# A new slot pipeline for two graph-attention layers: scores two chunks ahead, values two behind

## The reference

```
h = relu(layernorm(x)); x = x + L0(h, adj)      # scores q.k/sqrt(32) + beta*adj, masked where adj <= 0
h = relu(layernorm(x)); x = x + L1(h, adj)      # scores q.k/sqrt(384) + adj, then @ Wo.T + bo
q = h @ Wq; k = h @ Wk; v = h @ Wv              # L0 with biases on q, k, v; L1 with W.T and a bias on v
out = softmax(scores) @ v                        # L1: rows whose scores are all 0 give 0
```

## Time and profile before

| | |
|---|---|
| median of three runs | 2788.24 us |
| profiled execution: span from first to last instruction | 2786.6 us |
| PE busy | 2492.9 us, 89% |
| DVE busy | 2035.5 us, 73% |
| ACT busy | 2045.4 us, 73% |
| POOL busy | 1205.5 us, 43% |
| share of the DMA queue of SP (q1) | 33.7% |

### The profile page before, as it was taken

The page is one execution under the profiler, slowest core; times in us unless marked ns, Lnnn a source line. Parts: engine busy times, 40 slices in busy tenths (PEclk is TensorE's granted clock), DMA queues, the critical chain, the costliest instruction groups (busy, mean ns, idle before and its releaser), DMA issues.

```text
span 2786.6 us, 78169 instructions
## 1 busy us (share of the span) xinstructions
PE 2492.9 (89%) x20772; PEld 1447.7 (52%) x20772; DVE 2035.5 (73%) x10864; ACT 2045.4 (73%) x7824; POOL 1205.5 (43%) x1543
## 2 busy tenths in 40 slices
PE   3699999999999999999999999999999999999976
PEld 2355555555555555555555555555555555555543
DVE  3477777777777777777777777777777777777756
ACT  2577777777777777777777777777777777777765
POOL 1344444454444444444444444444444444444431
PEclk8899999999999999999999999999999999999988
DMA  3333333333333333333333333333333333333321
GB/s 118 90 89 87 93 94 87 95 102 86 88 96 86 94 103 86 86 97 87 94 102 88 85 99 86 94 100 89 83 99 88 95 98 90 82 99 91 78 55 45
DMA packets 164279, 251.27 MB, mean 90 GB/s; under 512 B 29776, under 2 KB 114768, under 8 KB 163920
## 3 DMA queue, kind: packets, MB, share of 16 engines
q1 hardware_dynamic: 163920, 248.11, 33.7%
HBM read 71.83 MB, written 25.17 MB: 35 GB/s over the span
## 4 chain that ended last, share of the span: by engine, by line
PE 45%; ACT 17%; DVE 16%; issue 16%; POOL 3%; SPq 1%; ACTq 1%; DVEq 1%; DMA 0%; POOLq 0%
PE job_bank L765 21%; ACT probs L479 12%; PE pt_bank L792 9%; PE o_bank L807 4%; PE misc_bank L832 4%; DVE neg L575 4%; PE score_bank L781 2%; PE misc_bank L846 2%; DVE stats L603 2%; ACT h_hi L516 2%; ACT probs_t L493 2%; PE misc_bank L868 1%; ACT qk L531 1%; DVE h_lo L700 1%; POOL part_lo L420 1%
## 5 line engine op out<-in xcount | busy, mean ns | idle before, releaser
L479 ACT ACTIVATE probs<-neg,neg_max 128x128 f32<-128x128 f32 x3072 | 1185.5, 390 | 9.4 <-DVE neg_max L575 9.4
L493 ACT ACTIVATE probs_t<-pt_bank 128x512 f32<-128x512 f32 x768 | 458.2, 597 | 567.7 <-PE pt_bank L792 516.5
L406 POOL TENSOR_TENSOR rstd<-shift_var,minus_half 128x1 f32<-128x1 f32 x256 | 152.2, 595 | 1020.3 <-DVE shift_var L612 1020.3
L479 ACT ACTIVATION_READ_ACCUMULATOR probs<-neg,neg_max 128x1 f32 x3072 | 583.9, 190 | 0.0
L792 PE MATMUL pt_bank<-ident,probs 128*128 128x128 f32 x3072 | 476.1, 278 | 57.5 <-ACT probs L479 42.9
L420 POOL TENSOR_TENSOR part_lo<-qk,part_hi 128x512 f16<-128x512 f32 x384 | 459.1, 1205 | 115.6 <-DVE part_hi L710 115.6
L792 PEld LDWEIGHTS pt_bank<-ident,probs 128*128 128x128 f32 x3072 | 362.7, 141 | 238.9 <-ACT probs L479 154.8
L765 PE MATMUL job_bank<-h_hi,w_hi 128*128 128x512 f16 x1152 | 441.4, 383 | 43.9 <-ACT qk L531 25.4
L765 PE MATMUL job_bank<-h_lo,w_hi 128*128 128x512 f16 x1152 | 438.5, 381 | 0.0
L765 PE MATMUL job_bank<-h_hi,w_lo 128*128 128x512 f16 x1152 | 438.0, 380 | 0.0
L575 DVE CUSTOM_DVE_ANT_0 neg<-score_bank,bias 128x128 f32<-128x128 f32 x1536 | 352.8, 285 | 103.3 <-issue 98.6
(11 more groups left out here) (69 smaller groups left out, 3949.8 us busy)
## 6 DMA issues: line engine op xcount, KB each, us to landing
stack<-part_hi SPq DMA_DIRECT2D x1024, 96.0 KB, 2.2
stack<-part_lo SPq DMA_DIRECT2D x512, 96.0 KB, 2.2
x_norm<-in_x SPq DMA_DIRECT2D x32, 768.0 KB, 4.5
x_res<-in_x SPq DMA_DIRECT2D x32, 768.0 KB, 4.7
out_x<-result SPq DMA_DIRECT2D x128, 192.0 KB, 1.9
adj<-in_adj SPq DMA_DIRECT2D x64, 256.0 KB, 2.9
stack<-in_L_gnn_Wq SPq DMA_DIRECT2D x2, 576.0 KB, 8.1
stack<-in_L_gnn_Wk SPq DMA_DIRECT2D x2, 576.0 KB, 8.9
```

What stands on the lines that cost most here:

```text
L406: pool.tensor_tensor(rstd[:, :], shift_var[:, b % 2, 1:2], minus_half[:, :], ALU.pow).then_inc(rstd_done, 1)
L479: last = act.activation(probs[c % 2][:, h, :], neg[c % 2][:, h, :], ACT.Exp, bias=neg_max[:, b, first + h:first + h + 1], scale=-1.0, accu ...
L493: act.activation(probs_t[c % 2][:, :, :].rearrange("p h q -> p (h q)"), pt_bank[c % 2][:, :], ACT.Copy).then_inc(probs_t_ready, 1)
```

## The change

Every engine's list of slots is rewritten; the arithmetic stays in the same form, apart from what is named here.

- PE: scores of chunk s+2 instead of s+1, the turn of chunk s-1 instead of s, and values of chunk s-2 instead of s-1. The mm of the projection are counted out per slot by a table (`PROJ`, one list for phases that attend layer 0, one for layer 1) and laid in three parts between the other work. The output projection comes at the slot's end.
- ACT: the exponentials of chunk s come first, the copy of chunk s-1 behind them. `part_hi` is written straight from PSUM at the slot's end. It also copies the turned inverse sums (`inv_t`) and writes `o_hi`; the copy `o_t` goes to DVE.
- DVE: `part_lo` straight from PSUM (one instruction instead of the cast), `o_t` or `o_norm` straight from `o_bank`, one instruction fewer for rows that are all zero, two instructions for layer 0's bias instead of three, built now in slot 11 of the layer-0 phase instead of slot 7 of the layer-1 phase.
- POOL no longer makes `part_lo`.
- PSUM: one `pt_bank` instead of two; `post_bank` and `h_bank` instead of `misc_bank`.
- Norms are at slots 0, 2, 4 and 6, turned two slots later and split three slots later, so that two are under way at a time.
- Scales: layer 0's weights for q and k are scaled by 16 instead of 256, and the factor is taken back in the scores.
- Start: layer 1's weights come already turned from the host, `x` and the first three matrices are loaded first, and the first phase of norms stands between the splits of the weights.

```diff
+PROJ = ((7, 7, 7, 6, 7, 7, 7, 6, 9, 9, 9, 9), (5, 8, 8, 4, 7, 8, 5, 9, 12, 6, 9, 9))
+MATMULS = 3 * KC
+
+NORM_SLOTS = (0, 2, 4, 6)
...
+    def counts(self):
+        return PROJ[self.attend.layer if self.attend is not None else 0]
+
+    def parts(self, s):
+
+        if self.project is None:
+            return (), (), ()
+        first = sum(self.counts()[:s])
+        todo = [divmod(m, MATMULS) for m in range(first, first + self.counts()[s])]
+        one = (len(todo) + 2) // 3
+        if s == SLOTS - 1:
+            one = (len(todo) + 1) // 2
+        return todo[:one], todo[one:2 * one], todo[2 * one:]
+
+    def jobs_done(self, s):
+
+        if self.project is None or s < 0:
+            return []
+        return [j for part in self.parts(s) for j, m in part if m == MATMULS - 1]
...
+                    u, b = finished(p, s, 5)
+                    if of_layer(u, b, 1):
+                        sp.wait_ge(result_ready, u.group * GROUP + (b + 1))
+                        sp.dma_start(out[u.group * GROUP + b, :, :], result[b][:, :]).then_inc(stored[b], 16)
+                    for j in p.jobs_done(s - 1):
+                        if j == KC - 1 or j == QK_JOBS - 1:
+                            stack(p.project, j // KC)
+                    if s == 6 and p.tail is not None and p.tail.layer == 0:
...
+            def high_part(u, j):
+                n = u.n * QK_JOBS + j
+                t = j // KC
+                act.wait_ge(job_done, u.n * JOBS + (j + 1))
+                if j % KC == 0 and some((u.half + u.parity) * STACK_DMAS * 16):
+                    act.wait_ge(stack_in[t][1 - u.parity], (u.half + u.parity) * STACK_DMAS * 16)
+                if u.layer == 0:
+                    last = act.activation(part_hi[t][:, j % KC, :], job_bank[j % 2][:, :], ACT.Identity,
+                                          scale=1.0, bias=b_cols[t][:, j % KC:j % KC + 1])
+                else:
+                    scale = (SCALE[1] if t == 0 else 1.0) / W_SCALE
+                    last = act.activation(part_hi[t][:, j % KC, :], job_bank[j % 2][:, :], ACT.Copy, scale=scale)
+                last.then_inc(part_hi_ready, 1)
...
+                    u, b = finished(p, s, 3)
+                    if of_layer(u, b, 1):
+                        act.wait_ge(inv_turned, u.group * GROUP + (b + 1))
+                        if some(u.group * GROUP + b):
...
+                        act.activation(inv_t[:, :, :].rearrange("p c q -> p (c q)"), post_bank[:, 0:DIM],
+                                       ACT.Copy).then_inc(inv_t_ready, 1)
+                    u, b = normed_in(p, s, 3)
+                    if u is not None:
+                        act.wait_ge(h_turned, u.n * GROUP + (b + 1))
...
+                        act.activation(h_hi[u.parity][:, :, P * b:P * (b + 1)],
+                                       h_bank[:, 0:DIM].rearrange("p (c n) -> p c n", c=KC),
+                                       ACT.Relu).then_inc(h_hi_ready, 1)
+                    if p.attend is not None:
+                        exponentials(p.attend, s)
                     u, c = unit_of_chunk(p, s - 1)
                     if u is not None:
...
-                        act.activation(probs_t[c % 2][:, :, :].rearrange("p h q -> p (h q)"), pt_bank[c % 2][:, :],
+                        act.activation(probs_t[c % 2][:, :, :].rearrange("p h q -> p (h q)"), pt_bank[:, :],
                                        ACT.Copy).then_inc(probs_t_ready, 1)
-                    if p.attend is not None:
-                        exponentials(p.attend, s)
-                    u, b = finished(p, s, 1)
...
-                    if p.project is not None and 1 <= s < 1 + 2 * KC:
-
-                        u, j = p.project, s - 1
-                        n = u.n * 2 * KC + j
-                        act.wait_ge(job_done, u.n * JOBS + (j + 1))
...
-                            last = act.activation(qk32[j % 2][:, :], job_bank[j % 2][:, :], ACT.Copy, scale=scale)
-                        last.then_inc(qk32_ready, 1)
...
+                    u, b = finished(p, s, 3)
+                    if of_layer(u, b, 1):
+                        act.wait_ge(o_norm_ready, u.group * GROUP + (b + 1))
+                        if some(u.group * GROUP + b):
+                            act.wait_ge(out_done, u.group * GROUP + b)
+                        act.activation(o_hi[:, :, :], o_norm[:, :, :], ACT.Copy).then_inc(o_hi_ready, 1)
+                    for j in p.jobs_done(s):
+                        if j < QK_JOBS:
+                            high_part(p.project, j)
+
+            high_weights(0, 3)
+            phase(before()[0])
+            high_weights(3, WEIGHTS)
+            act.wait_ge(cols_ready, 3)
+            run_phases(act, phase, 1)
...
+            def low_part(u, j):
+                t = j // KC
+                dve.wait_ge(part_hi_ready, u.n * QK_JOBS + (j + 1))
+                if u.layer == 0:
+                    last = dve.scalar_tensor_tensor(part_lo[t][:, j % KC, :], job_bank[j % 2][:, :],
+                                                    b_cols[t][:, j % KC:j % KC + 1], part_hi[t][:, j % KC, :],
...
             def phase(p):
-
-                bias_slot = SLOTS - 1 if p.attend is not None and p.attend.layer == 0 else 7
+                bias_slot = SLOTS - 1 if p.attend is not None else 7
                 for s in range(SLOTS):
+                    u, b = finished(p, s, 3)
+                    if of_layer(u, b, 0):
+                        dve.wait_ge(pv_done, chunk(u, b * KC + KC - 1))
...
+                        dve.tensor_copy(o_t[:, :, :].rearrange("p c q -> p (c q)"),
+                                        o_bank[:, 0:DIM]).then_inc(o_taken, 1)
+                    if of_layer(u, b, 1):
+                        dve.wait_ge(pv_done, chunk(u, b * KC + KC - 1))
+                        dve.wait_ge(inv_t_ready, u.group * GROUP + (b + 1))
+                        if some(u.group * GROUP + b):
+                            dve.wait_ge(o_lo_ready, u.group * GROUP + b)
+                        dve.tensor_tensor(o_norm[:, :, :].rearrange("p c q -> p (c q)"), o_bank[:, 0:DIM],
+                                          inv_t[:, :, :].rearrange("p c q -> p (c q)"),
+                                          ALU.mult).then_inc(o_norm_ready, 1)
+                    for j in p.jobs_done(s - 1):
+                        if j < QK_JOBS:
+                            low_part(p.project, j)
+                        else:
+                            take_v(p.project, j - QK_JOBS)
                     if p.bias is not None and s == bias_slot:
                         build_bias(p.bias)
-                    if p.project is not None and s in (8, 9, 11):
-                        take_v(p.project, {8: 0, 9: 1, 11: 2}[s])
                     u, c = unit_of_chunk(p, s + 1)
...
-                    if p.project is not None and 1 <= s < 1 + 2 * KC:
-
...
-                        dve.tensor_copy(part_hi[j // KC][:, j % KC, :], qk32[j % 2][:, :]).then_inc(part_hi_ready, 1)
-                    if p.project is not None and s == 11:
...
+                    u, b = normed_in(p, s, 0)
+                    if u is not None:
+                        norm_stats(u, b)
+                for j in p.jobs_done(SLOTS - 1):
+                    take_v(p.project, j - QK_JOBS)
...
             def phase(p):
                 for s in range(SLOTS):
-                    u, c = unit_of_chunk(p, s + 1)
+                    one, two, three = p.parts(s)
+                    u, c = unit_of_chunk(p, s + 2)
                     if u is not None:
                         scores(u, c)
-                    parts = range(3 * s, 3 * s + 3) if s < 2 * KC else range(2 * s + 6, 2 * s + 8)
-                    if p.project is not None:
-                        for part in parts[:1]:
-                            project(p.project, part)
+                    u, b = finished(p, s, 4)
+                    if of_layer(u, b, 0):
+                        turn_rows(u, b)
+                    for j, m in one:
+                        project(p.project, j, m)
                     u, c = unit_of_chunk(p, s - 1)
                     if u is not None:
+                        turn_probs(u, c)
+                    for j, m in two:
+                        project(p.project, j, m)
+                    u, c = unit_of_chunk(p, s - 2)
+                    if u is not None:
                         weigh_values(u, c)
+                    for j, m in three:
+                        project(p.project, j, m)
                     u, b = finished(p, s, 4)
-                    if u is not None and u.layer == 1:
-
-                        if p.norm is not None and some(p.norm.n * GROUP + s // KC):
-                            pe.wait_ge(h_lo_ready, p.norm.n * GROUP + s // KC)
-                        pe.wait_ge(o_hi_ready, u.group * GROUP + (b + 1))
-                        pe.wait_ge(o_lo_ready, u.group * GROUP + (b + 1))
```

(25 more changed lines are left out.)

479 lines of the change are left out of this document (213 added, 266 removed).

## The result

| | before | changed |
|---|---|---|
| median, us | 2788.03 (2783.97 to 2789.91, 4 runs) | 2914.82 (2912.14 to 2915.7, 4 runs) |
| span of the profiled execution, us | 2786.6 | 2912.2 |
| a turn of the loop / 28 turns / outside it, us | 83.45 / 2336.5 / 450.1 | 88.74 / 2484.7 / 427.5 |
| PE, DVE, ACT, POOL busy, us | 2492.9, 2035.5, 2045.4, 1205.5 | 2539.8, 2073.5, 2055.3, 719.3 |

The changed kernel is slower: ratio 1.0454, 95% interval 1.0439 to 1.0469. The forecast was 2777 us in a range of 2690 to 2835. Both halves missed to the same side: a turn takes 88.74 us where 84.4 stood (28 x 4.34 = 121 us), and outside the loop 23 us were won where 38 stood.

The account below looks back on a forecast made before the run. The path from k's last job through the stack's DMAs to the scores bounds each phase, plus clock falls: 84.4 us a turn. From 2786.6, +27 in the loop and -38 outside give 2775.6, +1.6 around the span: 2777 us, range 2690 to 2835.

Parts of the forecast that it names:

- The ring: From k's last projection job through 12 stack DMAs to slot 10's scores: sets phase length, PE waits 4.3 and 2.8 us.
- The clock: PE's clock falls behind each wait for the stack, costing 1.25 us per wait, bounds 0 and 1.7.
- Rival (a): PE waits for the stack, but 3 to 4 us don't lower its clock: about 2700 us, chance 0.20.
- VectorE in the layer-1 phase: Late negated scores in slots 2 to 5 and slot 7's output row add 1.4 us, bounds 0 and 4.
- rival (b): DVE paces the layer-1 phase and delays SP's k stack; 1.7 us more a turn gives 2825 us, chance 0.16.
- Layer-0 phase, slots 0 to 2: DVE grows to some 31 of 41 us in this phase and delays nothing, so no time was added.
- Outside the loop: Start, norm-only phases, last unit and six other phases together: -38 us.
- The start: Before the loop, norms beside weight loading and splitting, no weights turned on PE: -21 us, between 0 and -27.
- The six phases in the loop's manner: Phases outside the loop that follow the ring and its clock: +3 us, between -15 and +10.
- the two that only norm: Two phases outside the loop, two norms under way at once, 19 us to about 14: -10, between 0 and -16.
- the last unit: Attended without projection outside the loop, 43 us before: -10 us, between 0 and -16.
- Rival (c): Stacks don't bind through a shorter path to landing; PE bounds a turn at 73.4 plus 1.6 us: 2500 us, chance 0.12.

Follow-up runs that it names:

- e1: Changed kernel with projection matmuls dealt 9,9,9,9,9,9,6,6,6,6,6,6, so k's last job ends in slot 5 instead of 7: 2617.7 us, turn 79.3.
- e5: Changed kernel with TensorE's scores one chunk ahead instead of two, the new dealing kept: 2620.5 us, turn 79.3.
- e9: e6 with SyncE issuing the stack's 12 DMAs ahead of the output's DMA in slots that have both: 2708.8 us, turn 82.0.
- e2: Changed kernel with 60 and 36 extra 128x128 matmuls on TensorE in slot 10, ahead of its wait for the stack: 2800.8 us, turn 84.8.
- e4: Changed kernel without layer 1's row-wise absolute maximum on VectorE: 2810.8 us, turn 85.4.
- e6: Changed kernel with projection dealt 8,8,8,8,8,8,6,7,7,7,7,8 in both phases, so k's last job ends in slot 6: 2859.1 us, turn 86.7.
- e10: Changed kernel with its loop turned by one phase, so the back edge lies ahead of the phase with layer 1's attention: 2909.9 us, turn 88.7.
- e12: Changed kernel with the edits of e1 and e5 together, old dealing and scores one chunk ahead: 2595.5 us, turn 78.6.

## Why the prediction was wrong

- **The ring: right.** The waits stand where they were put, 4.2 and 2.9 us for 4.3 and 2.8, the path from issue to scores is 9.4 us in the layer-0 phase and 9.7 in the layer-1 phase for 9.4. e1 and e5 open it by two different edits, and e9 does so in the layer-1 phase.
- **The clock: the mechanism right, the size short. This is the first term of the sum that failed.** "I take 1.25 us for each wait; the bounds are 0 and 1.7" gave 2.5 us a turn; e2 measured 3.96, of which 2.1 stood behind the longer wait and 1.6 behind the shorter. The step took the 3.4 us at half speed of the earlier trace rows as the most there is. At the wait of 4.2 us it was 6.8 us in 17 of 20 turns; in the one shown 2.2 of them lie in the wait and 4.6 behind it. This is +1.5 us a turn. Rival (a) is refuted: the clock falls behind 2.9 us too. The Trainium skill, TensorE: Matmul & The Clock Gate, section "HAM oscillation — how this bites in real kernels", describes a loop in which the wait for a DMA brings the clock down anew each time; the trace agrees, in every turn and at both waits. The waits of 1.6 us in e5, as regular, did not bring it down.
- **VectorE in the layer-1 phase: right place, half the size. This is the second.** 1.4 us were put down, within 0 to 4; 2.9 were measured, and taking 7 us of its load away gives just these back (e4). Of the grounds named, the load was right and the output row wrong: it held the stack by 0.2 us, though in e6 it does so by 5.1. This is +1.5, near the 1.7 that rival (b) named; (b) alone would have given 2825.
- **Layer-0 phase, slots 0 to 2: the third, put at nothing.** "DVE grows to some 31 of 41 us and delays nothing": +1.05 us, although it is busy only 27.8. About 0.6 of it went when the back edge was moved (e10). The three terms make 4.0 of the 4.3 us.
- **Outside the loop.** -23 for -38. The start was near its -21: the first projection comes at 23.2 us instead of 53.0, and the first scores, now a slot earlier, at 58.4 instead of 79.7. The six phases in the loop's manner had +3; at half of a turn's miss, 2.2 us each, they account for 13 of the 15. e1 points the same way: with the ring open 394.7 us lie outside the loop instead of 427.5. How the shortfall divides between these phases, the two that only norm and the last unit was not traced.
- **Rival (c)** was right on what an open ring is worth in kind but not in size: the turn is 78.6 and not 75, and PE then waits 3.5 us in it for VectorE's output rows (e12).
- **What the prediction never asked** is what the change would be without its dealing. The three misses add up because they lie on one chain: in a closed ring each late step lengthens the phase in full. Why all three went to the same side the runs don't say; VectorE's 1.4 stood low in bounds of 0 to 4, and the third had no bounds.

## What to carry to other kernels

Before spreading work evenly, find which of it starts a slow path (here twelve DMAs, 10 us from job to landing) and put that part first; with scores two chunks ahead the even spread cost 297 us (25 with one), and the old front-loaded dealing with the new pipeline is 6.1% faster than the kernel before. Where a wait of 3 to 4 us recurs on TensorE, count it with the clock behind it: filling it with matmuls whose result is thrown away gave 4 us a turn (e2). And when a step moves, read which wait stands ahead of it in its queue at the new place: the same stack lost 5 us behind an output row, and its four last DMAs 4 us behind POOL's waits.
